# Gate weights carried with the dispatched rows, expert rows summed by accumulating gathers, bias rows and an earlier gate step, in an attention and mixture-of-experts kernel

## The reference

```python
xn = _layernorm(x)
x = x + attn(xn) + ffn(xn)
# attn: 16 heads of 128, causal; q is reshaped to (b, h, t, dh) without a transpose
logits = einsum('bhtd,bhds->bhts', q, k) * scale
out = softmax(logits + mask) @ v ;  return out @ Wo + bo
# ffn: shared part, and 6 of 64 experts for each token, 128 slots an expert
scores = sigmoid(x_flat @ w_gate);  _, topk_idx = top_k(scores, 6)
w = take(scores, topk_idx);  w = w / w.sum(-1)
x_disp = zeros(E, CAP, C).at[flat_e, pos].set(x_flat[token_ids], mode='drop')
g, v = split(einsum('ecd,edh->ech', x_disp, w_up))
out_r = einsum('ech,ehd->ecd', silu(g) * v, w_down)
routed = (out_r[flat_e, pos].reshape(N, 6, C) * w[:, :, None]).sum(1)
```

## Time and profile before

| what | value |
|---|---|
| median of 3 runs | 1931.96 us (1929.65 to 1937.21) |
| the profiled execution: time, span | 1928.67 us, 1926.9 us |
| PE, DVE busy | 86%, 80% of the span |
| ACT, POOL busy | 56%, 60% of the span |
| first attention part | from about 75 us to 1014 us |
| experts | 1014.9 us (first load) to about 1131 us (last store) |

### The profile page before, as it was taken

How to read it: one execution, slowest core, us unless ns; L and a number is a source line. 1 busy time by engine, 2 the same in 40 slices (tenths; PEclk the granted TensorE clock), 3 DMA queues, 4 the chain that set the end, 5 groups by cost and what they waited for, 6 DMA issues and landing times. The chain is left out here.

```text
span 1926.9 us, 49610 instructions
## 1 busy us (share of the span) xinstructions
PE 1666.5 (86%) x19088; PEld 1296.6 (67%) x19088; DVE 1536.8 (80%) x3189; ACT 1083.2 (56%) x2347; POOL 1154.6 (60%) x1004
## 2 busy tenths in 40 slices
PE   1589989999899999999876789998998989999996
PEld 1466777777667777777655767766676776677674
DVE  4888878888788888888854458988988898988885
ACT  0556566666566666656552236655665655566564
POOL 0156667777677777777660027666666666766653
PEclk8799999999999999999997589999999999999999
DMA  9266656565655555545557648777878778777865
GB/s 346 95 136 118 120 114 123 122 114 104 124 90 95 92 99 99 93 87 94 118 95 201 193 112 140 124 133 132 144 129 142 130 143 135 130 123 127 149 119 103
DMA packets 692723, 245.04 MB, mean 127 GB/s; under 512 B 643584, under 2 KB 680785, under 8 KB 691600
## 3 DMA queue, kind: packets, MB, share of 16 engines
q1 hardware_dynamic: 657344, 197.80, 56.1%
q0 software_dynamic: 18432, 33.64, 7.1%
q10 hardware_dynamic: 16720, 10.51, 1.9%
HBM read 57.11 MB, written 50.46 MB: 56 GB/s over the span
## 5 line engine op out<-in xcount | busy, mean ns | idle before, releaser
L476 POOL TENSOR_TENSOR prob<-prob 128x128 f16<-128x128 f32 (+7 forms) x512 | 662.5, 1297 | 626.9 <-ACT prob L856 620.2
L849 ACT ACTIVATE prob<-prob,nmax 128x128 f32<-128x128 f32 (+7 forms) x512 | 397.0, 775 | 644.3 <-DVE prob L1291 631.5
L687 PE MATMUL ps_s<-kT,qT 128*128 128x512 f16 (+3 forms) x2304 | 457.6, 326 | 7.3 <-DVE prob L1291 3.6
L702 PE MATMUL ps_o<-probT,vh 128*128 128x256 f16 (+1 forms) x3840 | 425.3, 264 | 6.5 <-DMA probT<-prob 5.8
L1291 DVE TENSOR_SCALAR_CACHE_REDUCE prob<-ps_s,neg_scale 128x128 f32<-128x128 f32 (+7 forms) x512 | 409.8, 808 | 2.9 <-PE ps_s L689 2.0
L702 PEld LDWEIGHTS ps_o<-probT,vh 128*128 128x128 f16 x3840 | 367.4, 99 | 50.7 <-issue 7.5
L856 ACT CAST prob<-prob 128x128 f16<-128x128 f32 (+7 forms) x512 | 341.5, 667 | 2.2
L687 PEld LDWEIGHTS ps_s<-kT,qT 128*128 128x128 f16 x2304 | 199.5, 98 | 147.0 <-issue 13.1
L716 PE MATMUL ps_y<-wo,oT 128*128 128x256 f16 x1536 | 210.8, 273 | 85.6 <-DVE oT L1306 58.5
L579 PE MATMUL ps_t<-xT,wq 128*128 128x64 f16 x6144 | 202.5, 195 | 61.8 <-DVE z L1193 22.9
L579 PEld LDWEIGHTS ps_t<-xT,wq 128*128 128x128 f16 x6144 | 193.3, 99 | 73.5 <-issue 33.2
(11 more groups left out here) (173 smaller groups left out, 1759.4 us busy)
## 6 DMA issues: line engine op xcount, KB each, us to landing
dispatched<-zeros SPq DMA_DIRECT2D x16, 512.0 KB, 14.8
probT<-prob SPq DMA_TRANSPOSE x512
ex<-dispatched SPq DMA_DIRECT2D x16, 512.0 KB, 4.5
expert_out<-eo ACTq DMA_DIRECT2D x16, 512.0 KB, 4.0
eup<-in_L_ffn_w_up_dram SPq DMA_DIRECT2D x64, 64.0 KB, 2.1
dispatched<-xn,slot_idx POOLq DMA_INDIRECT x192
xn_columns<-xnth SPq DMA_DIRECT2D x24, 128.0 KB
got<-expert_out,slot_idx POOLq DMA_INDIRECT x192
```

Source lines behind the costliest of these rows:

```text
L476: pool.tensor_tensor(low_cols(j), prob_cols(j).rearrange("p (r k) -> p r k", k=P), high_cols(j), ALU.subtract).then_inc(p_low, 1)
L687: pe.matmul(s_cols(j, lo, hi), qT[:, u, a, j * P:(j + 1) * P], kT[:, u, c, lo:hi], start=(n == 0), stop=(n == 2 and hi < w))
L702: mm = pe.matmul(ps_o[:, lo:2 * P], vh[:, u, a, r * D:(r + 1) * D], probT[:, PT_AT[c] + 2 * r + s, lo:], start=(r + n == 0), stop=(r == 2 ...
L849: nc.scalar.activation(prob_cols(j), prob_cols(j), ACT.Exp, bias=nmax[:, j:j + 1], scale=-1.0, accum_out=rsum[:, i % 2, j:j + 1]).then_inc ...
```

## The change

- **Gate weights.** The three operations that turn the top-8 logits into weights now run tile pair by tile pair in the odd heads: two exponent steps and three copies on ACT (`exp_weights`, `weights_plus_one`, `set_weights`), three small operations on DVE (`weight_sums`). Weights and expert numbers are written behind the 256 values of each row (268 columns), and are scattered with it. In the expert stage DVE finds the weight of each slot (`esel`, `ew`) and multiplies the hidden activations by it, one operation more for each group. The five operations at L1446 to L1454 are gone.
- **Gathers.** `gather(t, k)` adds onto an accumulator tile (`compute_op=ALU.add`), 8 tiles deep; ACT first fills it with the constant row (`clear`). Four tiles take turns, so that a tile's next gather is issued four blocks later, and waits for the one before. DVE adds each finished tile once: 32 operations instead of 224.
- **Order.** PE runs `gates` and `shared_down` ahead of the second half of `project_k`; ACT runs `copy_gates` ahead of `high_k(i, 1)`; DVE runs `take_logits` and `add_shared` ahead of `low_k(i, 1)`, `low_q(i, 1)` behind `block_max(i, 1)`, and `full_q` ahead of the indices and `chosen`. The expert loop is written out.
- **Biases** are loaded as 48 rows of 128 by SP and transposed by PE; `bvB`, `bqT` and `bkT` are copied from PSUM.
- **`scale_of_y`** is a tensor_scalar with an accumulator output instead of a tensor_tensor.

```diff
-            act.dma_start(bqT[:], bq.rearrange("(m d) -> d m", d=D)).then_inc(bias_in, 16)
...
+            sp.wait_ge(bias_zero, 1)
+            for n, b in enumerate((bq, bk, bv)):
+                sp.dma_start(bias_rows[n * H:(n + 1) * H, :], b.rearrange("(m d) -> m d", d=D)).then_inc(bias_in, 16)
...
+            pe.transpose(ps_o[:, 0:P], bias_rows[:], ident[:]).then_inc(bias_done, 1)
...
-            V.tensor_copy(bvB[:], bvT[:].unsqueeze(2).to_broadcast([P, H, P])).then_inc(bias_ready, 1)
+            V.tensor_copy(bvB[:], ps_o[:, 2 * H:3 * H].unsqueeze(2).to_broadcast([P, H, P])).then_inc(bias_ready, 1)
+            V.tensor_copy(bqT[:], ps_o[:, 0:H]).then_inc(bias_taken, 1)
...
             def gather(t, k):
-                if t > 1:
-                    pool.wait_ge(mix_step, (TOPK + 1) * (t - 2) + k + 1)
+                if k:
+                    pool.wait_ge(gathered[t % ACCS], 16 * (TOPK * (t // ACCS) + k))
+                else:
+                    pool.wait_ge(acc_set, t + 1)
                 pool.indirect_dma_start(
-                    out=got[:, t % 2, k, :], out_offset=None, in_=eout_d,
+                    out=acc[:, t % ACCS, :], out_offset=None, in_=eout_d,
...
+                            g, n = divmod(TB * (i - SPLIT) + j, GROUP * TOPK)
+                            if g < NT // GROUP:
+                                gather(GROUP * g + n % GROUP, n // GROUP)
...
+            def exp_weights(p):
+                act.wait_ge(top_step, 4 * p + 2)
...
+                nc.scalar.activation(wexp[:], v8[:, :, 0:TOPK], ACT.Exp, scale=-1.0).then_inc(w_exp, 1)
+            def weights_plus_one(p):
+                act.wait_ge(w_exp, 2 * p + 1)
+                nc.scalar.activation(wexp[:], wexp[:], ACT.Identity, bias=one_col[:]).then_inc(w_exp, 1)
...
+            def weight_sums(p, n):
+                if n == 0:
+                    dve.wait_ge(w_exp, 2 * p + 2)
+                    V.reciprocal(wexp[:], wexp[:]).then_inc(w_step, 1)
...
-                V.tensor_tensor(yscale[:], rinv[:], out_scale[:].to_broadcast([P, TB]), ALU.mult).then_inc(r_step, 1)
+                V.tensor_scalar(yscale[:], rinv[:], out_scale[:], None, ALU.mult, ALU.min, accum_out=yleast[:]).then_inc(r_step, 1)
...
-                    V.scalar_tensor_tensor(out=resid[:, t, :], in0=got[:, t % 2, k, :], scalar=gate_w[:, t, k:k + 1], in1=resid[:, t, :],
-                                           op0=ALU.mult, op1=ALU.add).then_inc(mix_step, 1)
...
+                V.tensor_tensor(resid[:, t, :], acc[:, t % ACCS, :], resid[:, t, :], ALU.add).then_inc(mix_step, 1)
...
+                    V.tensor_tensor(eh[:, u], eh[:, u], ew[:, u].unsqueeze(2).to_broadcast([P, EG, HE]), ALU.mult).then_inc(eh_step, 1)
```

More of the change, by code:

```diff
@@ L254, in causal_attention_with_moe @@
         eo_stored = sem("eo_stored")
-        gathered = [sem(f"gathered{u}") for u in range(2)]
+        ew_step = sem("ew_step")
+        acc_set = sem("acc_set")
+        gathered = [sem(f"gathered{u}") for u in range(ACCS)]
         mix_step = sem("mix_step")
@@ L314, in late_part, with mix_slot, mixed_by @@
             return i // 2 - 1 if i % 2 == 0 and 2 <= i <= ROWS else -1
+        def mix_slot(t):
+            return (t // GROUP + 1) * GROUP * TOPK + MIX_LAG + MIX_STEP * (t % GROUP)
+        def mixed_by(n):
+            return sum(mix_slot(t) <= n for t in range(NT))
         def turn(i, more):
@@ L436, in _ @@
             load_experts(0, True)
-            with sp.Fori(1, E // EG // 2) as g:
+            for g in range(1, E // EG // 2):
                 load_experts(g, False)
@@ L764, in attention @@
                     scores(i, 7)
-                    if more:
-                        project_k(i + 1, 1)
                     if even_part(i) >= 0:
@@ L770, in attention @@
                         shared_down(i, odd_part(i))
+                    if more:
+                        project_k(i + 1, 1)
                 for c in range(NC):
@@ L821, in _ @@
             experts(0, True)
-            with pe.Fori(1, E // EG // 2) as g:
+            for g in range(1, E // EG // 2):
                 experts(g, False)
@@ L981, in attention @@
                     high_probs(i, 6)
+                    if odd_part(i) >= 0:
+                        set_weights(odd_part(i))
+                    if i0:
+                        for t in range(ACCS, NT):
+                            if TB * (i - i0) <= mix_slot(t - ACCS) + 2 < TB * (i - i0 + 1):
+                                clear(t)
                     softmax_exp(i, 7)
@@ L1021, in _ @@
             experts(0, True)
-            with act.Fori(1, E // EG // 2) as g:
+            for g in range(1, E // EG // 2):
                 experts(g, False)
+            for t in range(ACCS):
+                clear(t)
             attention(SPLIT, B * H)
@@ L1347, in mix_at @@
                     def mix_at(j):
-                        n = TB * (i - i0) + j - MIX_LAG
-                        if mixing and 0 <= n < NT * (TOPK + 1):
-                            mix(n // (TOPK + 1), n % (TOPK + 1), NC * (i - 1) + j // 2)
+                        for t in range(NT if mixing else 0):
+                            if mix_slot(t) == TB * (i - i0) + j:
+                                mix(t, NC * (i - 1) + j // 2)
                     def mixed(j):
-                        return max(0, min(NT * (TOPK + 1), TB * (i - i0) + j - MIX_LAG + 1)) if mixing else 0
+                        return mixed_by(TB * (i - i0) + j) if mixing else 0
                     swap, even, odd, late = turn(i, more), even_part(i), odd_part(i), late_part(i)
                     block_max(i, 0)
-                    low_q(i, 1)
                     mix_at(0)
-                    low_k(i, 1)
                     if odd >= 0:
@@ L1371, in attention @@
                     block_max(i, 1)
+                    low_q(i, 1)
                     if odd >= 0:
@@ L1483, in _ @@
             experts(0, True)
-            with dve.Fori(1, E // EG // 2) as g:
+            for g in range(1, E // EG // 2):
                 experts(g, False)
             dve.wait_ge(eo_stored, 16 * E // EG)
-            dve.wait_ge(weight_ready, 1)
             dve.wait_ge(bd_added, NP)
```

156 lines of the change are left out of this document (97 added, 59 removed).

## The result

The changed kernel takes 1916.77 us (median of 4 runs, 1909.97 to 1917.84) against 1932.9 us: ratio 0.9906, 95% interval 0.988 to 0.9933. It is faster by 16 us. The forecast was 1892, a gain of 40.

What follows compares the result with a forecast made beforehand. It took a ring of DVE, ACT and POOL to set the first part's pace, and DVE, then PE, the second's. 1928.7 - 19.7 + 31 + 6 - 57 = 1889, plus 3.3 to the median, gave 1892 us, range 1830 to 1925.

Steps and rivals of the forecast that it cites:

- Start-up: Before the first head: root of the variance earlier, bias wait gone, copies slightly dearer; -19.7 us, bounds -10 and -22.
- First part: First attention part: moved `low_q` and the gate weights lengthen DVE's work in 16 pairs of heads; +31 us, bounds 0 and +40.
- a term of 1.05 x 16: First attention part: `low_q` behind the second maximum loses its cover in odd heads; +1.05 us a pair.
- The weights' term: First attention part, odd heads: three small DVE operations and a wait for ACT's exponent steps; +0.9 us a pair.
- Experts: Expert stage: one more operation for each of 16 groups, +5.3, plus small costs including `clear`; sum +6 us.
- Second part: Second attention part: shorter `yscale` and fewer mixes bring a head from 25.86 to 23.8 us; -57 over 28 heads.
- Its issue I price as the plain ones.: Second part, POOL: issuing an accumulating gather costs what a plain one does, with no wait for landing; 0 us.
- rival 3: POOL waits for its own accumulating gathers, holding the ring; 2088 us at a landing time of 16 us; chance 0.07.
- The `yscale` of 2.09 us becomes 0.25, -1.85: Second part, start of each head: the one-tensor-input form shortens DVE's `yscale`; -1.85 us a head.
- Rival 1: First part is bound by PE's wait at the head's start; -48 in place of +31, 1813 us; chance 0.2.
- Rival 2: Transfer engines fill up because an accumulating gather takes each twice as long; 1910 to 1925 us; chance 0.12.
- Rival 4: `yscale` doesn't get faster, leaving 2.05 - 1.5 a head in the second part; 1934 us, no change; chance 0.05.

Runs made afterwards that it cites:

- the last runs: Edits that paid, put together: two on the kernel before, 1864.65 and 1843.34 us; two on the changed kernel, 1824.2 and 1823.4 us.
- the mended changed kernel: Changed kernel with seven gathers a head, mixes behind blocks 0 and 6, `low_q` in its old place, `pick` and the column load ahead of block 7's steps: 1824.2 us.
- the mended kernel before: Kernel before with the new `scale_of_y`, the new bias rows and `pick` ahead of block 7's low half: 1843.34 us, ratio 0.9535.
- the repeated run: The changed kernel run once more, unedited, as base for other runs: 1911.05 us, ratio 0.9893.
- yscale alone: Kernel before with only the new `scale_of_y` (one tensor operand, a second output): 1897.06 us, ratio 0.9795.
- the split low half: Kernel before with POOL's low half of block 7 as two instructions of 512 columns instead of one of 1024: 1922.05 us, ratio 0.9948.

## Why the prediction was right and wrong

**Start-up**: right, -19.9 for -19.7, by its steps.

**First part**: +30.0 for +31. The run with `low_q` put back gives 14.0 us for a term of 1.05 x 16 = 17; a pair of heads falls by 1.12 us (54.91 to 53.79), and the two turns of sequences give 3.4 us back. So that term was sized rightly, though it fell on both heads of a pair. The weights' term of 14 was not measured by itself, and the last runs speak against it: a pair takes 51.41 us in the mended changed kernel, which carries the weights and the earlier gate step, and 51.86 in the mended kernel before, which has neither. Of the remaining 16 us, 4.3 lie in the two turns, which the forecast left out, and in the rest is the longer wait for `picked`, 18.1 - 8.1 = 10 us in 7 pairs, that I had read as a sink for other gains (DVE "reaches `slot_indices` 1.15 us too early anyway"). It was no sink: moving `pick` gives 17 us of the first part even in the kernel before (889.6 to 872.3). So the sum is right, its split only in part, and that the parts made up 31 was partly luck.

**Experts**: -3.5 for +6. A round grew from 13.0 to 13.4 us to 13.7 to 13.9, as the 0.66 said; the term failed by the granted clock. The kernel before had two rounds wholly at half clock, 16.6 us each, and the changed kernel had none; the sum had no term for that. The same 30 us of both kernels, before and then after:

```profile
1063.00:1078.00 15.00, 11.54 (x60) 10.19 (x60) 5.66 (x12) 2.78 (x7) 0.00 (x0) 0.50 0.53 155
1078.00:1093.00 15.00, 11.54 (x60) 10.20 (x59) 5.67 (x12) 2.78 (x7) 0.00 (x0) 0.50 0.52 152
```

```profile
1063.00:1078.00 15.00, 9.76 (x66) 8.48 (x66) 8.90 (x25) 3.57 (x9) 0.00 (x0) 0.77 0.72 208
1078.00:1093.00 15.00, 10.25 (x70) 8.62 (x70) 8.02 (x22) 3.70 (x9) 0.00 (x0) 0.74 0.69 202
```

The last number but two is the granted clock. 0.74 to 0.77 is a clock that goes to and fro between 0.50 and 1.00; 0.50 is one that stays low.

**Second part: the step that failed.** -23.7 for -57. It failed in three places.

1. "Its issue I price as the plain ones." It costs 1.64 us, not 1.07, which makes POOL's chain 4 to 4.5 us a head longer: 24.98 us, above the 23.8 of the forecast, and no gain elsewhere can show. Shown by the full POOL timeline, by the head of 25.0 that neither half the transfers nor yscale's form moves, by plain gathers (16 us faster) and by seven a head (10 us faster). The forecast looked at POOL only for a wait on the landing (rival 3), which lasts 5.5 us at the median and is never waited for, and not at whether POOL had room. It read "busy 136 of 200 us" as room enough and did not add up the head: eight gathers with their gaps, 8 x (1.64 + 0.16) = 14.4 us, and 10.2 us for the eight low halves at the lengths that they had before, 24.6 in all. With 1.07 for 1.64 the same sum gives 20.0, so at the forecast's price POOL would not have been the bound: the price of the issue is the step that failed.
2. "The `yscale` of 2.09 us becomes 0.25, -1.85". True to 0.01 us in the kernel before (25.86 to 24.00), and worth nothing in the changed one, where the old form takes 0.17 us. A DVE operation with two SBUF operands waits for the POOL instruction that it meets; the change had moved POOL's phase, so that at that moment POOL issues a gather. The term belonged to an alignment, not to a form. The wait didn't vanish either: `low_q`, which also has two SBUF operands, meets a low half now and takes 1.84 us at the mean over 1527 to 1703 us in the repeated run, 0.80 in its heads behind the gathers.
3. The turn of sequences, not in the sum: 27.54 to 32.89 us. PE comes to `project_q` earlier and the load of the columns, behind two transposes on SP, comes later. It rose in every kernel with faster heads (29.6 to 33.2 us; 30.8 with yscale alone). That the slower heads of before had covered it is my reading and not shown. That moving the load did not cure this turn is shown; which order would is open.

The shortfall adds up. The forecast took 2.05 us off each of 28 heads. 21 heads fell short of that by 1.2 us each, 25 in all; the turn rose by 5.35 instead, 7.4 short; the first gather head rose from 23.61 to 26.31, 4.8 short; the five heads behind the gathers kept to it; and the last interval, for which no gain was forecast, fell from 23.86 to 20.11. That is 25 + 7.4 + 4.8 - 3.8 = 33.4 of the 33.3 us missing.

**The rivals.** Rival 1 (first part bound by PE) is dead. Rival 2 named 1910 to 1925 us and the time fell there, by another cause: the doubling is real, the bound was not. Rival 3's wait never occurs; its landing time was right. Rival 4's premise was false. The other side, slower than before, came nowhere near. The kernel that the profile really called for, POOL full by issue, stood in no rival.

**What it was worth.** Two small edits, bias rows and `scale_of_y`, take the kernel before to 1864.65 us, 52 under the whole change. The rest of the change, above all the accumulating gathers and the new order of DVE, costs that back. Mended, they win again: 1824.2 us, 19 under the best version with the old gathers.

## What to carry to other kernels

Before moving work into a transfer that one engine issues, sum that engine's whole chain per iteration with the new issue time, and spread the transfers so that every iteration has room, since free time isn't carried over. When a tiny operation takes ten times its usual time, look at which instruction of the other engine ends with it: the gain from removing it holds only as long as the two meet. When several near-equal bounds stand behind one another, try the mends together: single trials show only the smaller part of each.

## What the hardware showed

- A DVE operation with two SBUF operands that starts while a POOL `tensor_tensor` runs ends behind it. The eight columns of yscale ended 0.02 to 0.04 us behind it in 45 of 45 cases of the kernel before (1.64 or 2.09 us, once 0.33) and in 45 of 45 with the split low half (0.67 or 1.12, once 0.33). Where they met none, or only POOL's issue of a gather (23 times in the changed kernel with the old form), they took 0.17. The form with one tensor operand took 0.21 to 0.22 us in all 64 heads of the run of yscale alone, at 1619.67 for one with POOL's low half running from 1619.54. The Trainium skill's "GPSIMD Engine Reference" (section "Key points") names such contention for two SBUF inputs; the trace agrees and shows it as a wait for the whole instruction.
- The 512 columns of `low_q`, 0.69 us when free, ended some 0.55 us behind the low half that held them, and a low half that starts after them can hold them too. One that starts 0.30 us later, in the repeated run:

```profile
1536.38 2.30 DVE L1351 TENSOR_TENSOR qT<-qf,qT 128x512 f16<-128x512 f32 x1
...
1536.68 1.43 POOL L497 TENSOR_TENSOR prob<-prob 128x384 f16<-128x384 f32 x1
```

- An accumulating indirect gather of 128 rows is recorded on POOL with 1.64 us at the mean against 1.07 for a plain one, puts the next POOL instructions 0.5 to 0.56 us later, and takes all 16 transfer engines 1.14 us against 0.52 to 0.65. Halving its bytes changed the last number only.
- In the expert stage PE was busy some 10 to 12 of 15 us, against 186.58 of 200 in the first part at a granted clock of 1.00, and its clock went to and fro between 0.50 (1.2 GHz) and 1.00 (2.4 GHz). The longest unbroken stretch at 0.50 differed between kernels: no long one in the changed kernel, 20 us with seven gathers, 37 before, 54 in the three runs that moved `pick` or the load alone. The stage took 160.1, 161.3, 163.6 and 169.0 to 170.2 us. So up to some 9 us of any comparison here may hang on that clock. What starts such a stretch was not tried.
